# A softmax unit's row of maxima: a DMA into the score operand in place of a TensorE product and a VectorE copy, with the score passes reordered

## The chip, the cores and the metric

The kernel runs on one core of a Trainium2 chip. The metric is the device time of one execution in microseconds (us); lower is better. The five engines of the core (TensorE, VectorE, ScalarE, GpSimd, SyncE; PE, DVE, ACT, POOL and SP in the profile) each run their own instruction stream in order and meet through semaphores.

## The reference

A layer norm of x (8 batches of 1024 rows, 128 columns), multi-query attention with 8 heads on it, and a linear feed-forward block:

```python
xn = _layernorm(x, axis=-1)
Q = jnp.einsum('bnd,hdk->bhnk', xn, proj_q)
K = jnp.einsum('bmd,dk->bmk', xn, proj_k)
V = jnp.einsum('bmd,dv->bmv', xn, proj_v)
weights = jax.nn.softmax(jnp.einsum('bhnk,bmk->bhnm', Q, K), axis=-1)
Y = jnp.einsum('bhnv,hdv->bnd', jnp.einsum('bhnm,bmv->bhnv', weights, V), proj_o)
out = x + Y + sum_e (xn @ w1[e]) @ w2[e]
```

## The kernel before, in words

The weights are folded at the start (query with key, value with output, and the feed-forward block into one matrix). After that the work is attention in float16 pairs: each operand is split into a high and a low half, and a product is three passes (high by high, high by low, low by high).

A batch and head is a *pair* (64 of them), a pair has two *blocks* of 512 queries, and a block has four *units* of 128 queries, so there are 512 units. Unit u belongs to block k = u // 4 and stands at place j = u % 4 in it. Its scores against all 1024 keys fill two PSUM banks as eight 128x128 products per pass. The softmax needs a maximum for each query. It is found from the high pass alone: VectorE reduces over key tiles (`max_of_keys`), TensorE turns the result (`turn_keys_max`), VectorE reduces again to a column with one negated maximum per query (`find_max`, L870). Since the scores have the keys on the partitions, that column must become a row: before, `max_to_row` (L636) turns it with an identity product into PSUM and `place_bias` (L878) copies the row into partition 0 of `g_lo`, where the second pass (`g_lo` by `x_hi`, whose first row is ones) adds it to every key. `low_passes(u)` runs the remaining 16 products in one place, after that bias.

TensorE walks through *periods*, n = 0 to 520. In period n it runs the high pass of unit n, the remaining passes of unit n-1, and two *chunks* of older work: a chunk is one key tile of the weighted sum of a block (`weigh`: products L654, L656 and L657, 512 columns each, called product 0, 1 and 2). Between them are `small_products`: a projection at place 1 (three 512-column products), the output product of a head (six small ones) at places 3 and 0, and a feed-forward tile in every eighth period (three small ones). By place n % 4 this order repeats every four periods; four periods are one block. The first key tile of a new block's sum is the second chunk of a period at place 2 (period 4m+2 starts the sum of block m-1). Its product 0 waits, in `weigh`, for all four low halves of that block's probabilities:

```python
if t == 0:
    pe.wait_ge(p_lo_ready, 4 * k + 4)
```

Once a unit's scores are complete (`scores_ready`), ScalarE takes the exponentials (L439) and rounds them to the high half (`p_high`, L446), and GpSimd computes the low half (`p_low`, L348). ScalarE's order has no high half at place 1 and two at place 2:

```python
if 1 <= n <= UNITS:
    exponentials(n - 1)
if at == 2 and 2 <= n <= UNITS + 1:
    p_high(n - 2)
if at != 1 and 1 <= n <= UNITS:
    p_high(n - 1)
```

GpSimd takes `p_low(n - 1)` in its iteration n, adds finished head outputs to the accumulator behind the low halves of the units at places 3 and 0 (`add_head`, L360), and in 54 of the 64 pairs normalises one tile for a later batch behind the low half of unit 8p (`normalise_next`, L342, with smaller parts at other places). SP's queue carries all input loads, the transposes of later tiles (`turn`) and the stores.

Of the kernel before, what the change touches and what calls it, by code (L numbers as in the profile page):

```python
# [11 lines left out]
P = 128  # L12
# [6 lines left out]
def attention_ffn(nc, x, wq, wk, wv, wo, w1, w2, out):  # L19
# [32 lines left out]
    with ctx:  # L52
# [6 lines left out]
        def sem(name):  # L59
# [32 lines left out]
        minus_max = sb("minus_max", [P, 2, P], F16)  # L92
# [39 lines left out]
        high_done, keys_max, turned, max_found, rowed, bias_ready = (  # L132
            sem(n) for n in ("high_done", "keys_max", "turned", "max_found", "rowed", "bias_ready"))
# [69 lines left out]
        def maxima_row(u):  # L203
            return turn_bank(u + 1)[:, 2 * P:3 * P]

# [49 lines left out]
        def _(sp):  # L255
# [11 lines left out]
            def turn(tile):  # L267

                batch = tile // NT
                at = tile % KEEP  # L270
                sp.wait_ge(xn_ready, tile + 1)
                if tile > NT:
                    sp.wait_ge(xT_in, turned_in(tile))
                if tile >= KEEP:

                    sp.wait_ge(scores_ready, (batch - 2) * 8 * H)
                    sp.wait_ge(ffn_ps, tile - KEEP + 1)
                sp.dma_start(xT[:, 0, at * P:(at + 1) * P], xn_hi[:, at, :], transpose=True).then_inc(xT_in, 16)
                sp.dma_start(xT[:, 1, at * P:(at + 1) * P], xn_lo[:, at, :], transpose=True).then_inc(xT_in, 16)
# [8 lines left out]
            for tile in range(NT, AHEAD):  # L288
                turn(tile)
            for pair in range(PAIRS):  # L290
                if (tile := ln_tile(pair - 1)) is not None:
                    turn(tile)

                if pair >= H + 1 and (pair - H - 1) % H == 0:
                    for half in range(2):
                        store((pair - H - 1) // H, half)
# [184 lines left out]
        def _(pe):  # L481
# [122 lines left out]
            def low_passes(u):  # L604

                k, j = divmod(u, 4)
                pe.wait_ge(bias_ready, u + 1)
                if j == 0:
                    pe.wait_ge(g_lo_ready, k + 1)
                for t in range(NT):  # L610
                    dst = bank(u, t // HT)[:, (t % HT) * P:(t % HT + 1) * P]
                    pe.matmul(dst, x_hi(batch_tile(k) + t), g_lo[:, k % 2, j * P:(j + 1) * P],  # L612
                              start=False, stop=False, skip_group_check=True)
                    last = pe.matmul(dst, x_lo(batch_tile(k) + t), g_hi[:, k % 2, j * P:(j + 1) * P],  # L614
                                     start=False, stop=True, skip_group_check=True)
                last.then_inc(scores_ready, 1)

            def turn_keys_max(u):
                pe.wait_ge(keys_max, u + 1)

                if u >= 1:
                    pe.wait_ge(bias_ready, u)
                if u == 7:
                    pe.wait_ge(f_copied, 1)
                if u == 4:
                    pe.wait_ge(w1_evacuated, E)
                pe.transpose(maxima_turned(u), key_max[:, u % 2, :], ident16[:, :]).then_inc(turned, 1)  # L627

            def max_to_row(u):
                pe.wait_ge(max_found, u + 1)  # L630
                if u == 3:
                    pe.wait_ge(w1_evacuated, E)

                if u % 4 == 2 and summing(u) >= 0:
                    pe.wait_ge(t_lo_ready, summing(u) + 1)
                pe.matmul(maxima_row(u), minus_max[:, u % 2, :], ident16[:, :], start=True, stop=True)\  # L636
                  .then_inc(rowed, 1)

            def weigh(k, t, first, rest):
# [5 lines left out]
                if first:  # L645
                    if t == 0:
# [4 lines left out]
                        pe.wait_ge(bias_ready, min(4 * k + 6, UNITS))  # L651
# [3 lines left out]
                if rest:  # L655
                    pe.matmul(dst, xn_hi[:, tile, :], p_lo, start=False, stop=False)  # L656
                    done = pe.matmul(dst, xn_lo[:, tile, :], p_hi, start=False, stop=t == NT - 1)  # L657
# [3 lines left out]
            def fold_ffn(e):  # L661
                if e == 0:
# [4 lines left out]
                    pe.wait_ge(bias_ready, 3)  # L667
# [353 lines left out]
```

## Time and profile before

| | us |
|---|---|
| median of 3 runs (1636.4 to 1636.76) | 1636.69 |
| the profiled execution | 1637.05 |
| its span in the profile | 1635.2 |

The profile is of one execution. TensorE is busy for 1618.8 us of the span, VectorE 1229.2, ScalarE 1300.6 and GpSimd 1379.3. TensorE's granted clock is 0.999 of full speed. A matmul's own duration in a timeline includes its way through the array; successive ones overlap, so the cost of one is read from the distance of the starts.

### The profile page before, as it was taken

To read this page: it belongs to the slowest core of one execution; us is meant where nothing else is said; L and a number is where in the kernel's file an instruction comes from. 1 tells how busy PE (TensorE), PEld (TensorE's weight loads), DVE (VectorE), ACT (ScalarE), POOL (GpSimd) and SP (SyncE) were. 2 spreads that over 40 slices of the span, in tenths; PEclk is the share of its full clock that TensorE was granted. 3 is DMA by queue.
4 is the path that set the end of the run, shared out by engine and by line. 5 is a ranking of instruction groups with operands and counts; after the bars stand their busy time and mean duration, and the time that the engine had idled before them with its cause. 6 is when DMAs were issued, how large, how long until landed. Compare 5 with 4: busy or idle time off the path is not lost.

```text
span 1635.2 us, 46288 instructions
## 1 busy us (share of the span) xinstructions
PE 1618.8 (99%) x18686; PEld 1199.7 (73%) x18686; DVE 1229.2 (75%) x2605; ACT 1300.6 (80%) x1348; POOL 1379.3 (84%) x1008
## 2 busy tenths in 40 slices
PE   8999999999999999999999999999999999999998
PEld 6777777777777777777777777777777777777775
DVE  6777777777777777777777777777777777777775
ACT  4788888888888888888888888888888888878885
POOL 3688888888888888888888888888888888888786
PEclk9999999999999999999999999999999999999999
DMA  8000000000000000000000000000000000000000
GB/s 237 4 3 5 5 4 18 4 4 5 4 17 5 4 5 5 16 5 5 4 5 18 3 5 5 4 18 4 4 5 3 18 5 3 4 14 2 2 2 14
DMA packets 34690, 20.41 MB, mean 12 GB/s; under 512 B 18353, under 2 KB 30897, under 8 KB 34481
## 3 DMA queue, kind: packets, MB, share of 16 engines
q1 hardware_dynamic: 33440, 16.92, 3.9%
q8 instruction: 152, 2.49, 0.6%
q10 hardware_dynamic: 1040, 0.52, 0.1%
q14 instruction: 58, 0.47, 0.1%
HBM read 9.57 MB, written 4.19 MB: 8 GB/s over the span
## 4 chain that ended last, share of the span: by engine, by line
PE 97%; DVE 1%; ACT 1%; issue 0%; ACTq 0%; POOL 0%; DVEq 0%
PE s_ps L599 14%; PE s_ps L614 14%; PE s_ps L612 14%; PE t_ps L654 13%; PE t_ps L657 13%; PE t_ps L656 13%; PE s_ps L483 4%; PE s_ps L485 4%; PE s_ps L484 4%; PE t_ps L636 2%; PE t_ps L627 1%; PE t_ps L669 0%; PE s_ps L627 0%; DVE c_lo L970 0%; ACT pr_hi L446 0%; DVE xn L772 0%
## 5 line engine op out<-in xcount | busy, mean ns | idle before, releaser
L348 POOL TENSOR_TENSOR pr_lo<-pr,pr_hi 128x1024 f16<-128x1024 f32 x511 | 1079.6, 2135 | 228.3 <-ACT pr_hi L446 228.3
L439 ACT ACTIVATE pr<-s_ps,boost,scale 128x1024 f32<-128x1024 f32 x512 | 616.4, 1204 | 193.7 <-PE s_ps L614 193.6
L865 DVE TENSOR_REDUCE key_max<-s_ps 128x128 f16<-128x1024 f32 x512 | 624.0, 1219 | 0.2 <-PE s_ps L599 0.2
L446 ACT ACTIVATE pr_hi<-pr 128x1024 f16<-128x1024 f32 x512 | 525.5, 1051 | 8.2
L612 PE MATMUL s_ps<-g_lo,xT 128*128 128x128 f16 x4096 | 512.4, 219 | 1.0 <-DVE g_lo L878 1.0
L614 PE MATMUL s_ps<-g_hi,xT 128*128 128x128 f16 x4096 | 512.4, 219 | 0.0
L612 PEld LDWEIGHTS s_ps<-g_lo,xT 128*128 128x128 f16 x4096 | 400.4, 98 | 31.5 <-DVE g_lo L878 1.5
L614 PEld LDWEIGHTS s_ps<-g_hi,xT 128*128 128x128 f16 x4096 | 400.5, 98 | 29.9
L654 PE MATMUL t_ps<-pr_hi,xn_hi 128*128 128x512 f16 x1024 | 388.2, 379 | 1.8 <-DVE pr_lo L883 1.8
L657 PE MATMUL t_ps<-pr_hi,xn_lo 128*128 128x512 f16 x1024 | 388.2, 379 | 0.0
L656 PE MATMUL t_ps<-pr_lo,xn_hi 128*128 128x512 f16 x1024 | 388.2, 379 | 0.0
L599 PEld LDWEIGHTS s_ps<-g_hi,xT 128*128 128x128 f16 x4096 | 287.5, 98 | 121.1 <-issue 1.2
L878 DVE CAST g_lo<-t_ps 1x128 f16<-1x128 f32 x512 | 142.8, 279 | 256.4 <-PE t_ps L636 256.4
L599 PE MATMUL s_ps<-g_hi,xT 128*128 128x128 f16 x4096 | 334.2, 219 | 0.1
L360 POOL TENSOR_TENSOR xacc<-xacc,y_tmp 128x256 f32<-128x256 f32 x255 | 187.1, 734 | 6.2 <-DVE y_tmp L898 6.1
L657 PEld LDWEIGHTS t_ps<-pr_hi,xn_lo 128*128 128x128 f16 x1024 | 100.1, 98 | 105.9
L861 DVE TENSOR_TENSOR g_lo<-s_ps,g_hi 128x512 f16<-128x512 f32 x127 | 87.8, 691 | 89.1 <-ACT g_hi L433 89.1
L452 ACT ACTIVATE t_hi<-t_ps 128x512 f16<-128x512 f32 x128 | 76.4, 597 | 89.8 <-PE t_ps L657 89.8
L898 DVE SCALAR_TENSOR_TENSOR y_tmp<-s_ps,scale,recip 128x256 f32<-128x256 f32 x256 | 123.8, 484 | 26.6
L870 DVE TENSOR_REDUCE minus_max<-t_ps 128x1 f16<-128x128 f16 x384 | 110.2, 287 | 5.9 <-PE t_ps L627 2.9
L636 PE MATMUL t_ps<-ident,minus_max 128*128 128x128 f16 x512 | 112.2, 219 | 0.7 <-DVE w1T L957 0.7
L656 PEld LDWEIGHTS t_ps<-pr_lo,xn_hi 128*128 128x128 f16 x1024 | 100.1, 98 | 15.7
(126 smaller groups left out, 1545.3 us busy)
## 6 DMA issues: line engine op xcount, KB each, us to landing
out_dram<-xacc SPq DMA_DIRECT2D x16, 256.0 KB, 2.7
w_sb<-in_L_ffn_w_dram SPq DMA_DIRECT2D x1, 2048.0 KB, 9.5
xT<-xn_hi SPq DMA_TRANSPOSE x56, 2.2
xT<-xn_lo SPq DMA_TRANSPOSE x56, 2.4
pr<-in_L_attn_proj_q_dram ACTq DMA_DIRECT2D x1, 512.0 KB, 4.6
xacc<-in_L_attn_x_dram SPq DMA_DIRECT2D x2, 256.0 KB, 5.0
pr<-in_L_attn_proj_o_dram SPq DMA_DIRECT2D x1, 512.0 KB, 6.5
xacc<-in_L_attn_x_dram SPq DMA_DIRECT2D x1, 384.0 KB, 10.4
```

The costliest lines, as they stand in the source:

```text
L348: pool.tensor_tensor(pr_lo[:, u % RING, :], pr32[:, u % PR, :], pr_hi[:, u % RING, :], ALU.subtract)\
L360: pool.tensor_tensor(acc, acc, y_tmp[:, g, :, :], ALU.add).then_inc(y_added, 1)
L439: act.activation(pr32[:, u % PR, :], both_banks(u), ACT.Exp, bias=boost[:, 0:1], scale=scale[:, 0:1])\
L446: act.activation(pr_hi[:, u % RING, :], pr32[:, u % PR, :], ACT.Copy).then_inc(p_hi_ready, 1)
L599: last = pe.matmul(dst[:, i * P:(i + 1) * P], x_hi(keys + i), g_hi[:, k % 2, j * P:(j + 1) * P], start=i == 0, stop=False, skip_group_chec ...
L612: pe.matmul(dst, x_hi(batch_tile(k) + t), g_lo[:, k % 2, j * P:(j + 1) * P], start=False, stop=False, skip_group_check=True)
L614: last = pe.matmul(dst, x_lo(batch_tile(k) + t), g_hi[:, k % 2, j * P:(j + 1) * P], start=False, stop=True, skip_group_check=True)
L636: pe.matmul(maxima_row(u), minus_max[:, u % 2, :], ident16[:, :], start=True, stop=True)\
L654: pe.matmul(dst, xn_hi[:, tile, :], p_hi, start=t == 0, stop=False)
L656: pe.matmul(dst, xn_hi[:, tile, :], p_lo, start=False, stop=False)
L657: done = pe.matmul(dst, xn_lo[:, tile, :], p_hi, start=False, stop=t == NT - 1)
L865: dve.tensor_reduce(key_max[:, u % 2, :], both_banks(u).rearrange("p (t q) -> p q t", q=P), AX_X, ALU.max).then_inc(keys_max, 1)
```

## The change

- `max_to_row` and `place_bias` are gone. `minus_max` shrinks to one column per unit, and SP's queue writes that column by a DMA as a row into partition 0 of `g_lo` (`bias(u)`; semaphore `bias_in`). Each such DMA waits for `find_max(u)` and for the one before it. `find_max(u)` waits for the DMA of unit u-2, whose column it overwrites.
- `low_passes(u)` is split into `low_keys` (`g_hi` by `x_lo`, no bias) and `low_queries` (`g_lo` by `x_hi`, with the bias). `low_keys` stays near the place of the old passes. `low_queries` comes after the period's second chunk at places 1, 2 and 3, and after product 0 of it at place 0.
- At place 1 the small products come before `low_keys`, elsewhere after it. At place 2 products 0 and 1 of the second chunk come before `turn_keys_max`, product 2 after it.
- On VectorE `find_max` comes ahead of `between_maxima` at places 1 and 2.
- SP issues its two transposes of a tile and its stores between the bias DMAs, each transpose behind a bias of its own.

ScalarE's and GpSimd's streams are unchanged. The diff, without declarations and helpers:

```diff
@@ -264,19 +261,29 @@
             sp.dma_start(w2_sb[:, :, :, :], w2.rearrange("e (c p) d -> p e c d", p=P)).then_inc(w2_in, 16)
             sp.dma_start(xacc[:, 2 * NT:TILES, :], x_tiles[:, 2 * NT:TILES, :]).then_inc(x_in[4], 16)
-            def turn(tile):
+            def bias(u):
+                k, j = divmod(u, 4)
+                sp.wait_ge(max_found, u + 1)
+                if j == 0:
+                    sp.wait_ge(g_lo_ready, k + 1)
+                if u >= 1:
+                    sp.wait_ge(bias_in, 16 * u)
+                sp.dma_start(g_lo[0:1, k % 2, j * P:(j + 1) * P], minus_max[:, u % 2:u % 2 + 1]).then_inc(bias_in, 16)
+            def turn(tile, half):
                 batch = tile // NT
                 at = tile % KEEP
                 sp.wait_ge(xn_ready, tile + 1)
-                if tile > NT:
-                    sp.wait_ge(xT_in, turned_in(tile))
+                if tile > NT or half > 0:
+                    sp.wait_ge(xT_in, turned_in(tile) + 16 * half)
                 if tile >= KEEP:
                     sp.wait_ge(scores_ready, (batch - 2) * 8 * H)
                     sp.wait_ge(ffn_ps, tile - KEEP + 1)
-                sp.dma_start(xT[:, 0, at * P:(at + 1) * P], xn_hi[:, at, :], transpose=True).then_inc(xT_in, 16)
-                sp.dma_start(xT[:, 1, at * P:(at + 1) * P], xn_lo[:, at, :], transpose=True).then_inc(xT_in, 16)
+                source = xn_lo if half else xn_hi
+                sp.dma_start(xT[:, half, at * P:(at + 1) * P], source[:, at, :], transpose=True).then_inc(xT_in, 16)
             def store(b, half):
                 k = 2 * (b * H + H - 1) + half
...
@@ -285,15 +292,18 @@
                 sp.wait_ge(y_added, 2 * k + 2)
                 sp.dma_start(out_tiles[:, first:first + HT, :], xacc[:, first:first + HT, :]).then_inc(stored, 16)
-            for tile in range(NT, AHEAD):
-                turn(tile)
-            for pair in range(PAIRS):
-                if (tile := ln_tile(pair - 1)) is not None:
-                    turn(tile)
-                if pair >= H + 1 and (pair - H - 1) % H == 0:
-                    for half in range(2):
-                        store((pair - H - 1) // H, half)
+            for u in range(UNITS):
+                bias(u)
+                pair, at = divmod(u, 8)
+                if pair == 1 and at in (4, 5, 6, 7):
+                    turn(NT + at // 2 - 2, at % 2)
+                if at in (1, 2) and pair >= 2 and (tile := ln_tile(pair - 2)) is not None:
+                    turn(tile, at - 1)
+                batch = pair // H - 1
+                if pair % H == 2 and at in (5, 6) and batch >= 0:
+                    store(batch, at - 5)
             for half in range(2):
                 store(B - 1, half)
             sp.wait_ge(stored, 16 * 2 * B)
...
@@ -601,59 +611,58 @@
                 if half == 1:
                     last.then_inc(high_done, 1)
-            def low_passes(u):
+            def low_keys(u):
                 k, j = divmod(u, 4)
-                pe.wait_ge(bias_ready, u + 1)
+                pe.wait_ge(keys_max, u + 1)
+                for t in range(NT):
+                    pe.matmul(bank(u, t // HT)[:, (t % HT) * P:(t % HT + 1) * P], x_lo(batch_tile(k) + t),
+                              g_hi[:, k % 2, j * P:(j + 1) * P], start=False, stop=False, skip_group_check=True)
+            def low_queries(u):
+                k, j = divmod(u, 4)
+                pe.wait_ge(bias_in, 16 * (u + 1))
                 if j == 0:
                     pe.wait_ge(g_lo_ready, k + 1)
                 for t in range(NT):
-                    dst = bank(u, t // HT)[:, (t % HT) * P:(t % HT + 1) * P]
-                    pe.matmul(dst, x_hi(batch_tile(k) + t), g_lo[:, k % 2, j * P:(j + 1) * P],
-                              start=False, stop=False, skip_group_check=True)
-                    last = pe.matmul(dst, x_lo(batch_tile(k) + t), g_hi[:, k % 2, j * P:(j + 1) * P],
-                                     start=False, stop=True, skip_group_check=True)
+                    last = pe.matmul(bank(u, t // HT)[:, (t % HT) * P:(t % HT + 1) * P], x_hi(batch_tile(k) + t),
+                                     g_lo[:, k % 2, j * P:(j + 1) * P], start=False, stop=True, skip_group_check=True)
                 last.then_inc(scores_ready, 1)
             def turn_keys_max(u):
                 pe.wait_ge(keys_max, u + 1)
                 if u >= 1:
-                    pe.wait_ge(bias_ready, u)
+                    pe.wait_ge(max_found, u)
                 if u == 7:
                     pe.wait_ge(f_copied, 1)
                 if u == 4:
                     pe.wait_ge(w1_evacuated, E)
+                if u % 4 == 3 and summing(u - 1) >= 0:
+                    pe.wait_ge(t_lo_ready, summing(u - 1) + 1)
                 pe.transpose(maxima_turned(u), key_max[:, u % 2, :], ident16[:, :]).then_inc(turned, 1)
-            def max_to_row(u):
-                pe.wait_ge(max_found, u + 1)
-                if u == 3:
-                    pe.wait_ge(w1_evacuated, E)
-                if u % 4 == 2 and summing(u) >= 0:
-                    pe.wait_ge(t_lo_ready, summing(u) + 1)
-                pe.matmul(maxima_row(u), minus_max[:, u % 2, :], ident16[:, :], start=True, stop=True)\
-                  .then_inc(rowed, 1)
-            def weigh(k, t, first, rest):
+            def weigh(k, t, products):
                 tile = (batch_tile(k) + t) % KEEP
                 at = (4 * k) % RING
                 p_hi, p_lo = pr_hi[:, at:at + 4, t * P:(t + 1) * P], pr_lo[:, at:at + 4, t * P:(t + 1) * P]
                 dst = sum_bank(k).rearrange("p (j c) -> p j c", j=4)
-                if first:
+                if 0 in products:
                     if t == 0:
                         pe.wait_ge(p_lo_ready, 4 * k + 4)
                         if k >= 2:
                             pe.wait_ge(t_lo_ready, k - 1)
-                        pe.wait_ge(bias_ready, min(4 * k + 6, UNITS))
+                        pe.wait_ge(max_found, min(4 * k + 6, UNITS))
                         if k == 1:
                             pe.wait_ge(f_copied, 1)
                     pe.matmul(dst, xn_hi[:, tile, :], p_hi, start=t == 0, stop=False)
-                if rest:
+                if 1 in products:
                     pe.matmul(dst, xn_hi[:, tile, :], p_lo, start=False, stop=False)
+                if 2 in products:
                     done = pe.matmul(dst, xn_lo[:, tile, :], p_hi, start=False, stop=t == NT - 1)
                     if t == NT - 1:
                         done.then_inc(pv_done, 1)
...
@@ -732,25 +740,29 @@
             fold_c(0)
             for n in range(PERIODS):
                 at = n % 4
                 if n < UNITS:
                     high_pass(n, 0)
-                if 1 <= n <= UNITS and at != 3:
-                    max_to_row(n - 1)
-                if n < UNITS:
                     high_pass(n, 1)
-                if 1 <= n <= UNITS and at == 3:
-                    max_to_row(n - 1)
                 if n == 0:
                     fold_c(1)
                 chunk(n, 0)
-                small_products(n)
+                if at == 1:
+                    small_products(n)
                 if 1 <= n <= UNITS:
-                    low_passes(n - 1)
+                    low_keys(n - 1)
+                if at != 1:
+                    small_products(n)
                 if at == 2:
-                    chunk(n, 1, rest=False)
+                    chunk(n, 1, (0, 1))
                 if n < UNITS:
                     turn_keys_max(n)
-                chunk(n, 1, first=at != 2)
+                chunk(n, 1, ((0,), (0, 1, 2), (2,), (0, 1, 2))[at])
+                if 1 <= n <= UNITS:
+                    low_queries(n - 1)
+                if at == 0:
+                    chunk(n, 1, (1, 2))
         @block.vector
         def _(dve):
...
@@ -759,11 +771,10 @@
             dve.memset(boost[:, :], LOG_BOOST).then_inc(slot_set, 1)
             dve.memset(c_hi[:, :, P:YW], 0.0).then_inc(slot_set, 1)
             dve.memset(c_lo[:, :, P:YW], 0.0).then_inc(slot_set, 1)
-            dve.memset(minus_max[:, :, :], 0.0).then_inc(slot_set, 1)
-            dve.wait_ge(slot_set, 6)
+            dve.wait_ge(slot_set, 5)
             dve.memset(c_hi[0:1, :, P:P + 1], 1.0).then_inc(slot_set, 1)
             dve.memset(ones_row[:, :], 1.0).then_inc(slot_set, 1)
-            dve.wait_ge(slot_set, 8)
+            dve.wait_ge(slot_set, 7)
             def tile_mean(slot):
                 dve.bn_aggr(mean_var[:, slot, :], stats[:, slot, :]).then_inc(ln_mean, 1)
...
@@ -867,15 +878,10 @@
             def find_max(u):
                 dve.wait_ge(turned, u + 1)
-                dve.tensor_reduce(minus_max[:, u % 2, 0:1], maxima_turned(u), AX_X, ALU.max, negate=True)\
+                if u >= 2:
+                    dve.wait_ge(bias_in, 16 * (u - 1))
+                dve.tensor_reduce(minus_max[:, u % 2:u % 2 + 1], maxima_turned(u), AX_X, ALU.max, negate=True)\
                    .then_inc(max_found, 1)
-            def place_bias(u):
-                k, j = divmod(u, 4)
-                dve.wait_ge(rowed, u + 1)
-                if j == 0:
-                    dve.wait_ge(g_lo_ready, k + 1)
-                dve.tensor_copy(g_lo[0:1, k % 2, j * P:(j + 1) * P], maxima_row(u)[0:1, :]).then_inc(bias_ready, 1)
             def p_low_last():
                 u = UNITS - 1
...
@@ -977,13 +983,14 @@
             g_low(0)
             for n in range(PERIODS):
-                if 1 <= n <= UNITS:
-                    place_bias(n - 1)
                 if n < UNITS:
                     max_of_keys(n)
-                between_maxima(n)
+                if n % 4 in (0, 3):
+                    between_maxima(n)
                 if n < UNITS:
                     find_max(n)
+                if n % 4 in (1, 2):
+                    between_maxima(n)
                 before_bias(n)
                 if n == UNITS + 1:
                     p_low_last()
```

## Rows read from the trace of the kernel before

**Rows 1.** The page: busy time by engine, and the chain that ended last by engine.
```profile
PE 1618.8 (99%) x18686; PEld 1199.7 (73%) x18686; DVE 1229.2 (75%) x2605; ACT 1300.6 (80%) x1348; POOL 1379.3 (84%) x1008
...
PE 97%; DVE 1%; ACT 1%; issue 0%; ACTq 0%; POOL 0%; DVEq 0%
```

**Rows 2.** The page: costliest groups; busy us, mean ns of one | idle before them, releaser.
```profile
L348 POOL TENSOR_TENSOR pr_lo<-pr,pr_hi 128x1024 f16<-128x1024 f32 x511 | 1079.6, 2135 | 228.3 <-ACT pr_hi L446 228.3
...
L446 ACT ACTIVATE pr_hi<-pr 128x1024 f16<-128x1024 f32 x512 | 525.5, 1051 | 8.2
...
L878 DVE CAST g_lo<-t_ps 1x128 f16<-1x128 f32 x512 | 142.8, 279 | 256.4 <-PE t_ps L636 256.4
...
L636 PE MATMUL t_ps<-ident,minus_max 128*128 128x128 f16 x512 | 112.2, 219 | 0.7 <-DVE w1T L957 0.7
```

**Rows 3.** Timeline of TensorE in a period at place 2: start us, us, engine, line.
```profile
818.75 0.22 PE L614 MATMUL s_ps<-g_hi,xT 128*128 128x128 f16 x1
818.81 0.38 PE L654 MATMUL t_ps<-pr_hi,xn_hi 128*128 128x512 f16 x1
819.03 0.22 PE L627 MATMUL s_ps<-ident,key_max 128*128 128x128 f16 x1
819.08 0.38 PE L656 MATMUL t_ps<-pr_lo,xn_hi 128*128 128x512 f16 x1
...
819.51 0.61 PE L599 MATMUL s_ps<-g_hi,xT 128*128 128x128 f16 x8
819.96 0.22 PE L636 MATMUL t_ps<-ident,minus_max 128*128 128x128 f16 x1
```

**Rows 4.** Timeline of ScalarE in the same period.
```profile
819.01 1.20 ACT L439 ACTIVATE pr<-s_ps,boost,scale 128x1024 f32<-128x1024 f32 x1 [0.30 <-PE s_ps L614]
820.12 1.99 ACT L446 ACTIVATE pr_hi<-pr 128x1024 f16<-128x1024 f32 x2
```

**Rows 5.** Timeline of GpSimd: two blocks, then the first and last block start used.
```profile
808.76 2.13 POOL L348 TENSOR_TENSOR pr_lo<-pr,pr_hi 128x1024 f16<-128x1024 f32 x1 [2.03 <-ACT pr_hi L446]
...
811.56 0.82 POOL L342 TENSOR_SCALAR xn<-xacc,mean_var,rstd 128x127 f32<-128x127 f32 x1
812.35 6.32 POOL L348 TENSOR_TENSOR pr_lo<-pr,pr_hi 128x1024 f16<-128x1024 f32 x3
...
821.24 2.14 POOL L348 TENSOR_TENSOR pr_lo<-pr,pr_hi 128x1024 f16<-128x1024 f32 x1 [0.97 <-ACT pr_hi L446]
...
824.01 6.31 POOL L348 TENSOR_TENSOR pr_lo<-pr,pr_hi 128x1024 f16<-128x1024 f32 x3
...
50.18 6.31 POOL L348 TENSOR_TENSOR pr_lo<-pr,pr_hi 128x1024 f16<-128x1024 f32 x3 [7.63 <-ACT pr_hi L446]
...
1614.39 2.13 POOL L348 TENSOR_TENSOR pr_lo<-pr,pr_hi 128x1024 f16<-128x1024 f32 x1 [1.90 <-ACT pr_hi L446]
```

**Rows 6.** Timeline of VectorE at place 3.
```profile
821.55 0.15 DVE L894 RECIPROCAL recip<-s_ps 128x2 f32<-128x2 f32 x1
821.81 0.48 DVE L898 SCALAR_TENSOR_TENSOR y_tmp<-s_ps,scale,recip 128x256 f32<-128x256 f32 x1
822.21 0.28 DVE L870 TENSOR_REDUCE minus_max<-t_ps 128x1 f16<-128x128 f16 x1
```

**Rows 7.** The page: the DMA queue, and two issues with median us to landing.
```profile
q1 hardware_dynamic: 33440, 16.92, 3.9%
...
xT<-xn_hi SPq DMA_TRANSPOSE x56, 2.2
...
xacc<-in_L_attn_x_dram SPq DMA_DIRECT2D x1, 0.5 KB, 25.7
```

**Rows 8.** Timelines near the start: SP's last load, and TensorE in period 1.
```profile
9.34 10.58 SPq L265 DMA_DIRECT2D xacc<-in_L_attn_x_dram  x1
...
25.65 0.22 PE L612 MATMUL s_ps<-g_lo,xT 128*128 128x128 f16 x1
...
27.05 0.39 PE L599 MATMUL s_ps<-g_hi,xT 128*128 128x128 f16 x4
```

More of the change, by code:

```diff
@@ L91, in attention_ffn @@
         key_max = sb("key_max", [P, 2, P], F16)
-        minus_max = sb("minus_max", [P, 2, P], F16)
+        minus_max = sb("minus_max", [P, 2], F16)
         pr32 = sb("pr32", [P, PR, N], F32)
@@ L131, in attention_ffn @@
         g_ps, g_hi_ready, g_lo_ready = sem("g_ps"), sem("g_hi_ready"), sem("g_lo_ready")
-        high_done, keys_max, turned, max_found, rowed, bias_ready = (
-            sem(n) for n in ("high_done", "keys_max", "turned", "max_found", "rowed", "bias_ready"))
+        high_done, keys_max, turned, max_found, bias_in = (
+            sem(n) for n in ("high_done", "keys_max", "turned", "max_found", "bias_in"))
         scores_ready, exp_done, p_hi_ready, p_lo_ready = (
@@ L201, in maxima_turned @@
             return turn_bank(u)[:, 0:P // 2].bitcast(F16)
-        def maxima_row(u):
-            return turn_bank(u + 1)[:, 2 * P:3 * P]
         def ffn_tile(n):
@@ L666, in fold_ffn @@
                     pe.wait_ge(max_found, 4)
-                    pe.wait_ge(bias_ready, 3)
                 for c in range(MC):
@@ L672, in fold_ffn, with chunk @@
                     last.then_inc(f_ps, 1)
-            def chunk(n, place, first=True, rest=True):
-                if n < 4 and rest:
+            def chunk(n, place, products=(0, 1, 2)):
+                if n < 4 and 2 in products:
                     turn_w1(2 * n + place)
-                if n in FOLDS and rest:
+                if n in FOLDS and 2 in products:
                     for e in range(2):
@@ L684, in chunk @@
                 if 0 <= k < BLOCKS:
-                    weigh(k, t, first, rest)
+                    weigh(k, t, products)
             def head_out(k, g):
```

## The prediction

> **What bounds the kernel now.** I read the page first. TensorE is busy for 99% of the span, and the chain that ended last is 97% TensorE [rows 1]. Hence anything taken off TensorE seems to be gain. But the next question is which loop lies closest behind it, since the change moves work. The groups show GpSimd with one large wait, for ScalarE's high half, 228.3 us in all [rows 2]. The timeline of GpSimd shows when: once in four periods, ahead of the low half of unit 4m. All other low halves follow back to back [rows 5].
>
> The step on TensorE is read from the starts. Eight small products take 819.51 to 819.96, so 0.0556 us each; from 819.08 to 819.51 two 512-column products take 0.215 each [rows 3]. A block of four periods has 104 small ones for scores, turns and rows, 12 for the head outputs (3 more for feed-forward in every second block) and 27 large ones: 116 x 0.0556 + 27 x 0.215 = 12.26 us, or 12.42. Measured are 126 blocks from the low half of unit 4 (50.18) to that of unit 508 (1614.39): 1564.2 us, 12.41 each [rows 5]. So TensorE nearly alone sets the block, with at most 0.07 us of waits.
>
> **The loop beside it.** Call W the start of product 0 of a new block's sum at place 2. It waits for four low halves. In order: the last score product of unit 4m+1 (818.75) releases the exponential (819.01), then comes the high half of unit 4m (820.12), then GpSimd starts the low half (821.24). That is 2.49 us [rows 3, 4, 5]. From there GpSimd needs 824.01 + 6.31 - 821.24 = 9.08 us to the end of the fourth low half, or, with a tile to normalise, 812.35 + 6.32 - 808.76 = 9.91 [rows 5]. Then W is free. Before, W stood one step behind the last score product (818.75, 818.81) [rows 3], so this loop had 2.49 + 9.91 - 0.06 = 12.34 us plus a wake-up: just hidden behind TensorE. The long case shows it: the low halves end at 818.67, W starts at 818.81. The cover is almost nil.
>
> **The change, part by part.**
>
> *Removed on TensorE:* one product per unit, 512 x 0.0556 = 28.5 us, 0.22 per block [rows 2, 3]. A block of TensorE work becomes 12.04 or 12.20 us. If nothing else bound, the kernel would gain 28 us.
>
> *Removed on VectorE:* the copy, 279 ns per unit [rows 2]. VectorE is not the bound, so this is worth nothing directly; it lets the key maximum start about 0.2 us earlier. Issuing `find_max` first at places 1 and 2 only moves it ahead of work of 0.69 us.
>
> *The pass with the bias moved to the end.* This is the term that decides. At place 2 the order is now product 0 (W), product 1, the turn, product 2, then the eight products of unit 4m+1 with the bias. From W to the last score product: 2 x 0.215 + 0.056 + 0.215 + 7 x 0.0556 = 1.09 us. Before it was -0.06, since the scores came first. The exponential of unit 4m+1, and in ScalarE's order the high half of unit 4m behind it, now start only after W. So the loop W to the next W is 1.09 + 2.49 + 9.08 + w = 12.66 + w, or 13.49 + w with a tile, where w is the wake-up of TensorE by GpSimd. Both exceed TensorE's 12.04 and 12.20. ScalarE's and GpSimd's orders don't change, and GpSimd's pieces stand back to back in it, so nothing closes up. TensorE will stand at W for 0.7 us in short blocks and 1.3 in long ones; behind it in its queue is everything else, the next maximum and the next scores with it.
>
> The trace shows no w. From below, 0.05: a product follows its predecessor by 0.056. From above, 0.26: TensorE wakes ScalarE in that time (818.75 to 819.01) [rows 3, 4]. I take 0.15, nearer the small step, because no result has to come through the array. Blocks: 12.81 and 13.64.
>
> *The DMA.* SP waits for `find_max(u)`, issues, and the row has to land before `low_queries(u)` nearly a period later. The covers, worked out with the steps above. At place 3 the key maximum and the head output (last product 1.81 us into the period) release VectorE at 2.07; the reciprocal, scaling and reduction take 0.26 + 0.40 + 0.28 [rows 6], so `find_max` ends at 3.01, where the period ends. `low_queries` at place 0 comes 2.13 us into the next: cover 2.1. The same sum gives 2.9, 2.8 and 2.7 us at places 1, 2 and 3. The nearest row is a transpose of 32 KB from SP, 2.2 us from issue to landing [rows 7]. The bytes here are 256, but they come from one element in each of 128 partitions, so in 128 pieces. The queue's packets took 3.9% of 16 x 1635.2 us over 33440, 30.5 ns each [rows 7]: 8 per engine add 0.25 us, 128 on one engine 3.9. From below I have no smaller row than the transpose; I bound it at 1.5, which would need no cover. I take 2.2, with 0.2 for the two handovers 2.4. The excess at place 0 is 0.3 us, and it costs nothing: TensorE has 12.81 - 12.04 = 0.77 us of idle time per short block at W, and a delay before W only shortens the stand there. With 0.13 us that the exponential of unit 4m+2 is late for the head output at place 0, about 0.6 us is left. So the DMA decides only from 2.9 us on. If the stand at W were gone, it would cost 0.3 x 128 = 38 us, more than the gain.
>
> The Trainium skill, "DMA: Bandwidth & Descriptors", section "Anatomy of one DMA", gives about 2.0 us fixed for one DMA; by that figure the row comes at 2.2 us and the sum is the same, since only the excess over 2.9 counts. The same page, section "Rules for kernel authors", says that a strided last dimension lowers to one descriptor per element: this speaks against the change, and it is the same as the 128 pieces above. No row here shows such a DMA.
>
> *SP's queue.* Each bias DMA waits for the one before, and transposes (2.2 us) and 16 stores stand between them; the next bias is due 3 us later, so they mostly clear. The column is free again (`find_max` waits for DMA u-2) a period early. The transposed tiles are needed a batch later. Nothing.
>
> *The start.* The DMA of unit 0 stands in the queue behind SP's last load, issued at 9.34 and landed 25.7 us later, at 35.0 [rows 7, 8]. Before, the pass of unit 0 started at 25.65 and period 2 at 27.05 [rows 8]. Now TensorE holds the last pass of period 1 until 35.1 and period 2 starts at 35.6: 8.5 us later. Later waits for the weights' transposition absorb some; I take 7, with 0 (if the queue let the row past) and 9 as bounds. The end changes by under 1 us, as the last low half is on VectorE in both.
>
> **The sum.** 72 short and 54 long blocks: 72 x 12.81 + 54 x 13.64 = 1658.9 us against 1564.2, so +94.7. With the start +102. On the profiled execution's 1637.05 (0.4 above the median of 1636.69) that is 1738.8: 1739 us. w between 0.05 and 0.26 gives -13 to +14, the start -7 to +2: its own range is 1719 to 1755.
>
> **Rivals.**
>
> *The DMA is late as well.* At 3.5 us from reduction to pass, the stands are about 0.8 at place 3, 0.5 at place 0, 0.15 at place 1 (each shortens the next cover's need): 12.17 + 1.4 = 13.6 for all blocks, +150 us, some 1795. At 3.1 it is 1754. For it: 128 pieces into one partition. Against: 0.25 us by the packets' mean. 14%.
>
> *One engine takes all 128 pieces.* Then 6.1 us per DMA, one after the other: 512 x 6.1 = 3100 us. For it: all pieces end in one partition. The Trainium skill, same page, section "Why a DMA increments its semaphore by 16 and not by 1", takes the number of engines from the slowest dimension above 1 of both sides; with 128 on both it would be 16, against this rival. 5%.
>
> *The row is hidden and TensorE stays the bound.* This is the faster side. It holds if W isn't held by the low halves: the loop would have to be 0.5 us shorter in short blocks, 1.3 in long ones, for instance if ScalarE gave unit 4m's high half before the exponential of 4m+1. Then 126 x 0.22 is gained, 1608 us, with the start 1616. For it: TensorE at 99%. Against: the order in the code and 818.67 beside 818.81. 7%.
>
> *It cancels:* a stand of 0.2 us per block in place of the rows, 1634 to 1640. 2%.
>
> The forecast itself has 72%. Leaving out the faster side and the one engine, the range is 1715 to 1800. A measurement of this kernel tells 0.2% (3.3 us) from no change: faster 0.07, within it 0.02, slower 0.91.
>
> **What the profile after should show.** TensorE's waits led by L654-like product 0 for GpSimd's low half, some 126 times and 0.7 to 1.5 us each, about 120 us in all. TensorE's busy share near 93%. GpSimd idle once per block, ahead of the low half of unit 4m, for 2.1 to 2.4 us (3.7 from W to that low half less 1.3 to 1.6 of head, feed-forward and tile work), and full otherwise. Blocks alternating 12.8 and 13.6 us, all short after the last normalised tile. `low_queries` of unit 0 at 35 us. If instead `low_queries` waits for the DMA in most periods, the second case holds; if no wait stands at W, my loop is wrong and with it the sign.

## The result, and the profile after

The changed kernel takes 1752.79 us (median of 4 runs, 1751.89 to 1753.71) against 1636.59 us: a ratio of 1.0709, 95% interval 1.0696 to 1.0722, so 116.2 us slower. The forecast was 1739 with 1715 to 1800.

From the page of the changed kernel: busy time and chain by engine (these answer to [rows 1]), three groups ([rows 2]), the new DMA's issue and the DMA queues ([rows 7]).

```profile
PE 1641.1 (94%) x18174; PEld 1148.9 (66%) x18174; DVE 1143.3 (65%) x2092; ACT 1274.2 (73%) x1348; POOL 1378.6 (79%) x1008
...
PE 66%; DMA 22%; issue 5%; DVE 5%; ACT 1%; DVEq 0%; ACTq 0%; POOL 0%
...
L358 POOL TENSOR_TENSOR pr_lo<-pr,pr_hi 128x1024 f16<-128x1024 f32 x511 | 1078.9, 2132 | 345.9 <-ACT pr_hi L456 345.4
...
L662 PE MATMUL t_ps<-pr_hi,xn_hi 128*128 128x512 f16 x1024 | 388.0, 379 | 27.7 <-issue 26.1
...
L629 PE MATMUL s_ps<-g_lo,xT 128*128 128x128 f16 x4096 | 316.0, 220 | 64.8 <-DMA g_lo<-minus_max 64.4
...
g_lo<-minus_max SPq DMA_DIRECT2D x512, 0.2 KB, 2.8
...
q1 hardware_dynamic: 107168, 17.09, 6.0%
q8 instruction: 147, 2.41, 0.6%
```

TensorE has 512 instructions fewer and is busy for 94% of a longer span. The chain now goes through the DMA for 22%. The page doesn't name GpSimd as what product 0 of the sum (L662) waits for; it has 26.1 us there as "issue", which is idle time without a releaser that the profile shows. The loop has to be read from the timelines. GpSimd, as in [rows 5]:

```profile
799.77 4.22 POOL L358 TENSOR_TENSOR pr_lo<-pr,pr_hi 128x1024 f16<-128x1024 f32 x2
...
807.66 2.13 POOL L358 TENSOR_TENSOR pr_lo<-pr,pr_hi 128x1024 f16<-128x1024 f32 x1 [2.08 <-ACT pr_hi L456]
...
810.44 6.31 POOL L358 TENSOR_TENSOR pr_lo<-pr,pr_hi 128x1024 f16<-128x1024 f32 x3
816.69 0.74 POOL L370 TENSOR_TENSOR xacc<-xacc,y_tmp 128x256 f32<-128x256 f32 x1
...
820.49 2.13 POOL L358 TENSOR_TENSOR pr_lo<-pr,pr_hi 128x1024 f16<-128x1024 f32 x1 [2.54 <-ACT pr_hi L456]
...
824.10 6.30 POOL L358 TENSOR_TENSOR pr_lo<-pr,pr_hi 128x1024 f16<-128x1024 f32 x3
...
834.08 2.13 POOL L358 TENSOR_TENSOR pr_lo<-pr,pr_hi 128x1024 f16<-128x1024 f32 x1 [2.08 <-ACT pr_hi L456]
```

Two blocks last 820.49 - 807.66 = 12.83 and 834.08 - 820.49 = 13.59 us; before they lasted 12.31 (blocks without a tile to normalise) and 12.48 (with one) in the median. TensorE around it, as in [rows 3]:

```profile
804.09 0.38 PE L662 MATMUL t_ps<-pr_hi,xn_hi 128*128 128x512 f16 x1 [0.62 <-issue]
...
810.37 0.38 PE L662 MATMUL t_ps<-pr_hi,xn_hi 128*128 128x512 f16 x1
811.12 0.62 PE L629 MATMUL s_ps<-g_lo,xT 128*128 128x128 f16 x8 [0.37 <-DMA g_lo<-minus_max]
...
816.23 0.38 PE L666 MATMUL t_ps<-pr_hi,xn_lo 128*128 128x512 f16 x1
...
816.89 0.38 PE L662 MATMUL t_ps<-pr_hi,xn_hi 128*128 128x512 f16 x1
...
817.32 0.22 PE L645 MATMUL s_ps<-ident,key_max 128*128 128x128 f16 x1
```

At 803.99 (799.77 + 4.22) the fourth low half ends and 0.10 us later, at 804.09, product 0 of the sum starts. TensorE had been through the work ahead of it since 803.30 (802.85 plus eight products of 0.056): it stands idle for 0.79 us. At place 0 it stands again: product 0 starts at 810.37 and would leave at 810.585, but the pass with the bias starts at 811.12, 0.53 us later, released by the DMA. The next W, at 816.89, comes without a stand: `low_keys` runs up to it (816.44 plus 0.45), while the low halves end at 810.44 + 6.31 = 816.75. In short blocks both limits meet. The maximum that this DMA carries was reduced here (VectorE, as in [rows 6]):

```profile
807.99 0.28 DVE L883 TENSOR_REDUCE minus_max<-t_ps 128x1 f16<-128x128 f16 x1
```

It ends at 808.27, so from reduction to pass are 2.85 us. The start, in windows (each row: its bounds and length, busy us of TensorE, its weight loads, VectorE, ScalarE, GpSimd, then TensorE's granted clock, the DMA engines' share and GB/s), and TensorE's own rows:

```profile
20.00:25.00 5.00, 4.12 (x33) 2.70 (x31) 4.74 (x9) 2.76 (x5) 0.00 (x0) 1.00 1.06 294
25.00:30.00 5.00, 1.15 (x14) 0.85 (x12) 2.17 (x6) 0.72 (x2) 0.00 (x0) 1.00 1.05 292
30.00:35.00 5.00, 0.00 (x0) 0.00 (x0) 0.00 (x0) 0.00 (x0) 0.00 (x0) 0.51 0.68 183
35.00:40.00 5.00, 4.65 (x36) 4.53 (x37) 1.57 (x3) 1.80 (x2) 0.00 (x0) 0.50 0.02 0
40.00:45.00 5.00, 2.88 (x37) 2.56 (x35) 2.21 (x4) 3.58 (x4) 2.09 (x2) 0.96 0.03 0
45.00:50.00 5.00, 5.00 (x61) 4.91 (x59) 3.33 (x4) 3.45 (x3) 4.88 (x4) 1.00 0.03 3
```

```profile
25.55 0.61 PE L558 MATMUL t_ps<-ident,w_sb 128*128 128x128 f32 x4
35.35 1.04 PE L629 MATMUL s_ps<-g_lo,xT 128*128 128x128 f16 x8 [9.20 <-DMA g_lo<-minus_max]
...
44.81 0.61 PE L629 MATMUL s_ps<-g_lo,xT 128*128 128x128 f16 x8
```

TensorE stands from 26.2 to 35.35 us, until the first bias DMA has come through behind the last load [rows 7, 8]. The granted clock is down to 0.51 in the last half of that stand, and at 0.50, the 1.2 GHz level, when work comes back: the same eight products take 1.04 us at 35.35 and 0.61 at 44.81.

GpSimd's rows for the first and the last block start used:

```profile
61.95 2.13 POOL L358 TENSOR_TENSOR pr_lo<-pr,pr_hi 128x1024 f16<-128x1024 f32 x1 [8.63 <-ACT pr_hi L456]
...
1730.62 2.13 POOL L358 TENSOR_TENSOR pr_lo<-pr,pr_hi 128x1024 f16<-128x1024 f32 x1 [3.17 <-ACT pr_hi L456]
```

The difference by place: the low half of unit 4 starts at 61.95 (before 50.18), that of unit 508 at 1730.62 (1614.39) [rows 5]. So 11.8 us arise at the start, 1668.7 - 1564.2 = 104.5 in the 126 blocks, and nothing at the end.

### The profile page after: what moved, and what is told of

The parts are those of the page before. It is cut to its first block, busy times and chain, and to the rows that moved or that the text cites. A ratio compares the mean times of both kernels' runs of the same rounds, so it can differ in the third digit from the quotient of the medians.

```text
span 1751.5 us, 46123 instructions
## 1 busy us (share of the span) xinstructions
PE 1641.1 (94%) x18174; PEld 1148.9 (66%) x18174; DVE 1143.3 (65%) x2092; ACT 1274.2 (73%) x1348; POOL 1378.6 (79%) x1008
## 3 DMA queue, kind: packets, MB, share of 16 engines
q1 hardware_dynamic: 107168, 17.09, 6.0%
## 4 chain that ended last, share of the span: by engine, by line
PE 66%; DMA 22%; issue 5%; DVE 5%; ACT 1%; DVEq 0%; ACTq 0%; POOL 0%
DMA g_lo<-minus_max 22%; PE s_ps L629 11%; PE s_ps L609 10%; PE s_ps L619 10%; PE t_ps L664 9%; PE t_ps L666 9%; PE t_ps L662 8%; PE s_ps L495 2%; PE s_ps L493 2%; PE s_ps L494 2%; DVE minus_max L883 2%; DVE recip L900 1%; DVE y_tmp L904 0%; PE t_ps L645 0%; PE t_ps L677 0%
## 5 line engine op out<-in xcount | busy, mean ns | idle before, releaser
L662 PE MATMUL t_ps<-pr_hi,xn_hi 128*128 128x512 f16 x1024 | 388.0, 379 | 27.7 <-issue 26.1
L629 PEld LDWEIGHTS s_ps<-g_lo,xT 128*128 128x128 f16 x4096 | 245.7, 98 | 203.4 <-DMA g_lo<-minus_max 169.1
L629 PE MATMUL s_ps<-g_lo,xT 128*128 128x128 f16 x4096 | 316.0, 220 | 64.8 <-DMA g_lo<-minus_max 64.4
L619 PEld LDWEIGHTS s_ps<-g_hi,xT 128*128 128x128 f16 x4096 | 272.1, 98 | 120.0 <-ACT pr L449 0.3
L609 PE MATMUL s_ps<-g_hi,xT 128*128 128x128 f16 x4096 | 312.7, 219 | 1.3 <-DVE inv_scale L807 1.1
L619 PE MATMUL s_ps<-g_hi,xT 128*128 128x128 f16 x4096 | 312.7, 219 | 0.0
L609 PEld LDWEIGHTS s_ps<-g_hi,xT 128*128 128x128 f16 x4096 | 255.9, 98 | 32.3 <-issue 1.7
L662 PEld LDWEIGHTS t_ps<-pr_hi,xn_hi 128*128 128x128 f16 x1024 | 100.2, 98 | 36.5 <-issue 33.0
L493 PE MATMUL s_ps<-c_hi,t_hi 128*128 128x130 f16 x512 | 99.8, 220 | 1.6 <-DVE t_lo L894 1.4
L495 PE MATMUL s_ps<-c_hi,t_lo 128*128 128x130 f16 x512 | 99.8, 220 | 0.0
L494 PE MATMUL s_ps<-c_lo,t_hi 128*128 128x130 f16 x512 | 99.8, 220 | 0.0
```

The source lines that it names most:

```text
L609: last = pe.matmul(dst[:, i * P:(i + 1) * P], x_hi(keys + i), g_hi[:, k % 2, j * P:(j + 1) * P], start=i == 0, stop=False, skip_group_chec ...
L619: pe.matmul(bank(u, t // HT)[:, (t % HT) * P:(t % HT + 1) * P], x_lo(batch_tile(k) + t), g_hi[:, k % 2, j * P:(j + 1) * P], start=False, s ...
L629: last = pe.matmul(bank(u, t // HT)[:, (t % HT) * P:(t % HT + 1) * P], x_hi(batch_tile(k) + t), g_lo[:, k % 2, j * P:(j + 1) * P], start=F ...
L662: pe.matmul(dst, xn_hi[:, tile, :], p_hi, start=t == 0, stop=False)
```

## The experiments

The kernel before ran beside each (1636.4 to 1636.6 us). All but the changed kernel are single executions.

**The order alone.** The kernel before, with the passes placed as in the changed kernel and the row still made by TensorE and VectorE:

```diff
+                if 1 <= n <= UNITS:
+                    low_keys(n - 1)
...
-                    low_passes(n - 1)
...
+                chunk(n, 1, ((0,), (0, 1, 2), (2,), (0, 1, 2))[at])
+                if 1 <= n <= UNITS:
+                    low_queries(n - 1)
+                if at == 0:
+                    chunk(n, 1, (1, 2))
```

> The kernel before with only the order of the passes changed: the score passes are split and the one with the bias goes last, as in the changed kernel, but the row of maxima is still made by TensorE's product and VectorE's copy, with no DMA. Theory (the loop through the late pass, ScalarE and GpSimd): the blocks are those of the changed kernel, 12.8 us, and 13.6 with a tile to normalise, and the start is undisturbed: 1637 + 93 = 1730 us (1722 to 1740). Rival (the DMA is the cost): no loop of this kind, 1632 to 1642.

Measured: 1730.64 us, +94.0. The chain that ended last, from the page, and the timelines of GpSimd and, for W, of TensorE:

```profile
PE 84%; DVE 12%; issue 3%; ACT 1%; ACTq 0%; POOL 0%; DVEq 0%
```

```profile
798.15 4.23 POOL L348 TENSOR_TENSOR pr_lo<-pr,pr_hi 128x1024 f16<-128x1024 f32 x2
...
806.06 2.13 POOL L348 TENSOR_TENSOR pr_lo<-pr,pr_hi 128x1024 f16<-128x1024 f32 x1 [2.48 <-ACT pr_hi L446]
...
819.65 2.13 POOL L348 TENSOR_TENSOR pr_lo<-pr,pr_hi 128x1024 f16<-128x1024 f32 x1 [2.08 <-ACT pr_hi L446]
```

```profile
802.48 0.38 PE L659 MATMUL t_ps<-pr_hi,xn_hi 128*128 128x512 f16 x1
```

The low halves end at 798.15 + 4.23 = 802.38 and W follows at 802.48, 0.10 us later. The long block is 819.65 - 806.06 = 13.59 us; the short ones are 12.75 to 12.78 throughout, but for the first one of all (15.51). With a wake-up of 0.10 the loop of the prediction gives 12.76 and 13.59. TensorE's share of the chain is 84%, from 97 before [rows 1]; GpSimd isn't on it by name here either. So the order alone, without any DMA, costs 94 of the 116 us, and the loop gives the length of its blocks.

**GpSimd's tile work out of the loop.**

```diff
                             .then_inc(ln_rstd, 1)
-                    if n % 8 == 1:
-                        normalise_next(tile)
+                        normalise_next(tile)
```

> The changed kernel with GpSimd's normalisation of a tile issued one iteration earlier, behind the reciprocal root, where GpSimd waits for ScalarE anyway. Theory (loop): the 54 long blocks of 13.58 us become like the short ones, 12.8 to 13.0: 31 to 42 us less, 1711 to 1722. Rival (TensorE's waits for the DMA set the blocks): the work was not on the path, 1748 to 1755.

Measured: 1719.25 us, 33.5 less than the changed kernel. An instruction of 0.83 us on an engine that is busy for 79% of the span is worth 0.6 us each time, since it stands on the loop. It isn't the whole 0.83 because the other limit takes over: from the third on, all blocks now last 12.8 to 13.7 us, as the short ones did.

**The high half first.**

```diff
-                if at == 2 and 2 <= n <= UNITS + 1:
-                    p_high(n - 2)
-                if at != 1 and 1 <= n <= UNITS:
+                if 1 <= n <= UNITS:
                     p_high(n - 1)
```

> The changed kernel with ScalarE computing the high half of a unit at place 0 of its block right behind its own exponential in the period at place 1, in place of behind the next unit's exponential at place 2. The loop from the start of a new sum to the next is cut, and the low halves are in time. Theory: the stand at product 0 of the sum goes; what is left is TensorE's 12.04 or 12.20 us and the DMA's lateness at place 0, with the measured 2.8 us of landing some 0.8 us: blocks of 12.9 and 13.05, 1719 us (1705 to 1730). If the loop alone had cost time, and the DMA were covered, 1626. If neither: 1753.

Measured: 1724.82 us. TensorE around W:

```profile
813.87 0.61 PE L617 MATMUL s_ps<-g_hi,xT 128*128 128x128 f16 x8
814.32 0.38 PE L660 MATMUL t_ps<-pr_hi,xn_hi 128*128 128x512 f16 x1
...
814.80 0.38 PE L664 MATMUL t_ps<-pr_hi,xn_lo 128*128 128x512 f16 x1
815.59 0.62 PE L627 MATMUL s_ps<-g_lo,xT 128*128 128x128 f16 x8 [0.40 <-DMA g_lo<-minus_max]
```

W at 814.32 follows `low_keys` (813.87 plus 0.45) at once: the stand at W is gone. In its place TensorE waits 0.57 us for the DMA (814.80 plus 0.215 to 815.59). Only 28 us come back. One reason is that the DMA's lateness lay hidden in the same idle time. A second one is in VectorE's waits of this kernel; it is the wait that is looked at below, with two DMAs in flight:

```profile
DVE t_lo L892 <- ACT t_hi L462: 63.8, 126, 2.5
```

The high half moved to place 1 makes ScalarE late with `t_hi` once in each block; the changed kernel has one such wait in all (2.5 us, near the start). VectorE's key maximum comes later by it, and TensorE's turn of it waits (34.9 us in 118 weight loads, a wait that the changed kernel doesn't list). I didn't separate the two reasons here.

**The last load cut up.** The 3 MB load goes in six parts, each behind a bias DMA.

```diff
-            sp.dma_start(xacc[:, 2 * NT:TILES, :], x_tiles[:, 2 * NT:TILES, :]).then_inc(x_in[4], 16)
...
+                if u % 4 == 1 and 2 <= (b := u // 4 + 1) < B:
+                    sp.dma_start(xacc[:, b * NT:(b + 1) * NT, :], x_tiles[:, b * NT:(b + 1) * NT, :])\
+                      .then_inc(x_in[4], 16)
```

> The changed kernel with the last input load (3 MB) cut into six loads of one batch, each issued behind the bias DMA of a unit at place 1 from unit 5 on, so that the first bias DMA no longer stands behind it in the queue. Theory (queue order, and TensorE's half clock after its 9 us stand): period 2 starts where it did before, 1752.8 - 11.5 = 1741 us (1739 to 1744). Rival (the stand at the start is absorbed later or has another cause): 1750 to 1755.

Measured: 1744.68 us, 8.1 less, just outside what I had given. Unit 4's low half is back from 61.95 to 53.26, so the row's way behind the load, with the lower clock after it, is shown as the main part of the start's loss (8.7 of 11.8 us). The order alone loses 2.8 us at the start as well (unit 4's low half at 53.0 in the first experiment), which this edit can't return.

**The DMA alone**, with the passes in the old order:

```diff
+                small_products(n)
+                if 1 <= n <= UNITS:
+                    low_keys(n - 1)
+                    low_queries(n - 1)
+                if at == 2:
+                    chunk(n, 1, (0,))
+                if n < UNITS:
+                    turn_keys_max(n)
+                chunk(n, 1, (1, 2) if at == 2 else (0, 1, 2))
```

> The changed kernel with its DMA and the passes in the old order: both remaining score passes of unit n-1 ahead of the turn of unit n. Now the maximum, the DMA and the pass with the bias stand in one ring: 0.45 us of pass, 0.06 turn, 0.26 and 0.29 to the reduced maximum, 2.8 landing, 0.1 handovers, 3.9 us per unit and 15.8 per block. Theory: 1637 + 126 x 3.4 = 2065 us (2000 to 2130). Rival (the row is covered wherever it stands, the order alone is what costs): 1620 to 1650.

Measured: 2078.46 us, 15.82 us per block (expected 15.8). The late pass is what gives the DMA its cover: without it the DMA costs 442 us.

**All covers together:** the high half first, the load cut up, and `find_max` ahead of `between_maxima` at every place.

> The changed kernel with the high half first (as in the run before), the loads split, and the second reduction ahead of the head and feed-forward scaling on VectorE at places 3 and 0 as well, which gives the DMA at place 0 0.6 us more. Theory (each DMA counts against its own cover of 2.7 to 3.4 us): blocks of 12.4, 1637 us (1625 to 1655). Rival (the DMAs are serial, each waits for the one before to land, 2.9 to 3.0 us per unit whatever the cover): blocks stay near 12.6 or above, 1660 to 1700.

Measured: 1684.48 us. My number is missed by 47 us; the figure fits the rival, serial DMAs. The next kernel tests that:

```diff
-                if u >= 1:
-                    sp.wait_ge(bias_in, 16 * u)
+                if u >= 2:
+                    sp.wait_ge(bias_in[u % 2], 16 * (u // 2))
```

> As the kernel before it in this call, but with two semaphores, so that a bias DMA waits only for the one two units earlier and two may be in flight. If the serial issue costs, this is 10 to 50 us faster than that kernel; if only each DMA's own 2.8 us count, the two are within 5 us. Theory: about 1620 us (1608 to 1640).

Measured: 1680.31 us, 4.2 less, on one execution of each, and 60 above the 1620 that I had given. So the serial issue isn't the cause either. ScalarE, VectorE and TensorE of this kernel in one block:

```profile
815.95 1.06 ACT L459 ACTIVATE pr_hi<-pr 128x1024 f16<-128x1024 f32 x1
816.91 0.58 ACT L465 ACTIVATE t_hi<-t_ps 128x512 f16<-128x512 f32 x1
```

```profile
816.74 0.29 DVE L884 TENSOR_REDUCE minus_max<-s_ps 128x1 f16<-128x128 f16 x1 [0.36 <-PE s_ps L646]
817.53 0.69 DVE L895 TENSOR_TENSOR t_lo<-t_ps,t_hi 128x512 f16<-128x512 f32 x1 [0.49 <-ACT t_hi L465]
818.13 1.22 DVE L877 TENSOR_REDUCE key_max<-s_ps 128x128 f16<-128x1024 f32 x1
```

```profile
818.32 0.61 PE L620 MATMUL s_ps<-g_hi,xT 128*128 128x128 f16 x8
...
819.41 0.23 PE L646 MATMUL t_ps<-ident,key_max 128*128 128x128 f16 x1
```

The high half at 815.95 now stands ahead of `t_hi` (816.91). VectorE waits 0.49 us for it, the key maximum starts only at 818.13, and TensorE, through with its work at about 819.10 (818.32 plus fourteen small products), turns it at 819.41. My remedy for one wait had made another, 0.3 us per block:

```profile
PEld t_ps L646 <- DVE key_max L877: 39.7, 127, 0.9
```

**The last cover too:** the pass at place 0 behind the whole chunk, and the tile work moved.

> As the kernel before it in this call, with the pass with the bias behind the whole second chunk at place 0 too (0.43 us more cover) and GpSimd's normalisation moved into its gap. Theory: TensorE's work of 12.04 or 12.20 us per block is all that is left, 1606 us (1600 to 1622), under the kernel before the change. Rival (exponentials come too late for the head outputs or the low halves): 1625 to 1650.

Measured: 1708.27 us, slower than the kernel before it and beyond both expectations. From the list of waits (us in all, times, longest):

```profile
PEld s_ps L493 <- ACT pr L451: 75.8, 125, 0.7
```

The head outputs wait 75.8 us for exponentials, 18.9 in the kernel before it. TensorE's weight loads wait less for the DMA (29.6 us, 52.0 before): one wait was exchanged for another, for ScalarE. Two edits went in together; the next kernel keeps the tile work, takes back the other and changes ScalarE's order.

**`t_hi` ahead of the high half:**

```diff
+                if at == 2 and 2 <= n <= UNITS + 1:
+                    p_high(n - 2)
                 if 1 <= n <= UNITS:
                     exponentials(n - 1)
-                if 1 <= n <= UNITS:
+                if at != 1 and 1 <= n <= UNITS:
                     p_high(n - 1)
```

> As the kernel with two DMAs in flight, but with ScalarE's order at place 2: the high half of the finished sum, then the high half of the unit at place 0, then the exponential; and GpSimd's normalisation in its gap. Explanation of why the two kernels before fell short (12.5 and 12.8 us per block in place of 12.25): the high half of the unit at place 0, done at place 1, delays the high half of the finished sum, that delays VectorE's low half of it, and that the key maximum of place 3, for which TensorE's turn stands 0.3 us. Theory: this stand goes from every block, 1680 - 35 = 1645 us (1635 to 1662). Rival (the DMA's scatter is what is left): 1675 to 1685.

Measured: 1654.75 us, in the range given and 25.6 less than the kernel with two DMAs in flight. From that kernel it differs by the tile work too, so the 25.6 us aren't shown to be ScalarE's order alone; the wait of 39.7 us shown above is down to 1.8. The list of waits has what is left (weight loads of TensorE):

```profile
PEld s_ps L631 <- DMA g_lo<-minus_max: 89.3, 299, 1.5
...
PEld s_ps L647 <- DVE key_max L878: 35.6, 125, 0.3
```

It is the best of these kernels and 98 us under the changed one, but still 18 above the kernel before. Its blocks are 12.56 us on average, against 12.04 or 12.20 of TensorE work. No version that I tried beats the kernel before.

## Why the prediction was right

**The loop.** Right, in place and size. W to the last score product 1.09, then 2.49, then 9.08 or 9.91, and a wake-up: I took 0.15, measured is 0.10. Forecast 12.81 and 13.64 us, measured 12.77 and 13.58 where no DMA interferes. The first experiment shows it alone, the second that GpSimd's work is on it, the third that it opens with ScalarE's order.

**The DMA's time.** Mis-sized: 2.4 us from reduction to pass, measured 2.85, with 2.8 of them from issue to landing. The nearest row I had, a transpose with 2.2, was too low. The pieces were not the reason (below). The bound of 2.9 from which it would decide was about right: at 2.85 the stand of 0.53 us at place 0 just fills TensorE's idle time, so the short blocks have both limits at once. That the DMA came to lie just under this bound was luck; I had priced it by a transpose, and nothing in the rows spoke for 2.85 rather than the 3.1 or 3.5 of the second case.

**The DMA's scatter.** Missing in the sum. With both limits met nothing is left for a late one. Over the 126 blocks the changed kernel takes 1668.7 us against 1655.0 with the order alone, 13.7 more. The 54 long blocks hide most of it (they still last 13.58 us, with few exceptions), and the first block is no measure (15.60 us, 15.51 with the order alone). The other 71 short blocks last 12.94 us in the mean, where the order alone has 12.77. How much of that is scatter can be read from the landing of the DMA of the unit at place 3, for which the pass at place 0 waits. In 10 of the 71 it landed more than 3.0 us after its issue; they last 13.33 us in the mean, the other 61 last 12.87. So the late DMAs make somewhat under half of the loss, and the rest is a tenth of a us in every short block, where the two limits meet.

What the late ones have in common is in the packets of the trace. Behind the first, 41 of the 511 bias DMAs landed later than 3.0 us. During each of the 41 a packet of 16 KB went through the queue that the profile's page calls "q8 instruction", and they landed 0.91 to 1.18 us after its end. The 301 DMAs that met no packet of the instruction queues (q8, q14) all landed within 2.85 us. Transposes and stores don't explain them: 138 bias DMAs were in flight together with one, only 5 of them late. From the DMA view of two stretches, one late DMA (issued at 187.76, landed 3.46 us later) and the one of the pass at 811.12, which has no line for q8:

```profile
q1 hardware_dynamic: 144, 0.00, 2.5%
q8 instruction: 1, 0.02, 1.7%
```

```profile
q1 hardware_dynamic: 144, 0.00, 2.7%
```

Over all nine traces with this DMA it is much the same: of 327 late ones 312 met such a packet, and the 15 others, in the kernels with the load cut up, were in flight together with a part of that load. The longest landing with two in flight, 4.0 us, is one of these. No run changed the instruction traffic, so this is a coincidence in time and not a tested cause; and 171 of the 511 met a q8 packet, so most of those weren't late.

**The start.** Mis-sized: 7 us, measured 11.8. The row did wait behind the load until 35.3. I had let later waits absorb some of it; instead the order added 2.8 us of its own and TensorE ran at the lower clock level for some 5 us after its stand, which I had not considered. By my estimate that is about 2.5 us (the eight products from 36.18 to 37.03 take 0.85 us, and 0.445 at full clock).

**The sum.** Start 4.8 us too low, long blocks 3.2 too high, short ones 13.0 too low (12.99 with the first, whose length alone gives 2.8): 14 of 1753.

**What the profile was to show.** TensorE at 93%: 94%. Blocks alternating 12.8 and 13.6: yes. Product 0 leading the waits with 120 us: not so in the list. About 0.5 us of the idle time per block is spent at the DMA instead of at W, and what stays at W is shown as "issue" or not at all. Of the rivals, the late DMA was half true: its delay was in the second case's direction but at the threshold; one engine for all pieces didn't happen (2.8 us to landing, not 6.1).

The Trainium skill, "DMA: Bandwidth & Descriptors", section "Anatomy of one DMA", has about 2.0 us of fixed cost per DMA, for DMAs that GpSimd issues; this one is issued by SP, and here the measured 2.8 us decides. What the Trainium skill, same page, section "Rules for kernel authors", says of a strided last dimension, one descriptor per element, agrees with the packets counted below. The advice against it weighs little here, as the pieces take 9 ns each.

## What to carry to other kernels

An engine at 99% busy says what a removed instruction can gain, not what a moved one costs. Before moving work later on it, follow the loop through the other engines back to it, with their program order, and compare its length with the period: here 12.34 of 12.4 us was in use in the blocks with a tile to normalise, and 1.15 us of delay came out almost whole in them (12.48 to 13.58); in the others 11.51 of 12.3 us was in use, and less than half came out (12.31 to 12.77). A DMA in place of two short instructions needs some 3 us of cover at every place in the period, plus room for its scatter; making that cover by reordering moves the delay into other loops, as three of the last four experiments showed.

## What the runs showed of the hardware

- A DMA of 256 bytes in SBUF, from 128 partitions into one, lands 2.8 us after its issue in the median (2.7 at least), more than a transpose of 32 KB in the same kernel (2.3). SP is busy 0.47 us with its issue.
- Its 128 pieces cost almost nothing: the queue has 107168 packets instead of 33440, so 144 per DMA, and their time rose from 3.9% of 16 x 1635.2 us to 6.0% of 16 x 1751.5 us, by 661 us for 73728 packets, 9 ns each. I had used 30.5.
- The bias DMAs that landed later than 3.0 us, 41 of 511 in the changed kernel, all had a packet of the queue "q8 instruction" beside them; the 301 that had none of q8 or q14 landed within 2.85 us.
- A DMA of 256 bytes issued at 22.85 us behind a load of 3 MB in the same queue landed at 35.3 us.
- After 9.2 us without work TensorE's granted clock was 0.50 for about 5 us of work, then full again.
